# Token table of a mixture of experts: neighbouring places 64 bytes apart, rows gathered with 8 KB

## What is computed

```
logits = xf @ router_w.T                       # 2048 tokens, 8 experts
topk_vals, topk_idx = jax.lax.top_k(logits, 2)
topk_w = jax.nn.softmax(topk_vals, axis=-1)
order = jnp.argsort(exp_id)
x_sorted = xf[order // K]                      # tokens brought together by expert
y1 = ragged_dot(x_sorted, w1, counts); gate, up = split(y1, 2)
y2 = ragged_dot(silu(gate) * up, w2, counts)
y = (y2[inv] * exp_w[:, None]) summed over the 2 experts of a token
```

## Time and profile before

| what | us |
|---|---|
| median of 3 runs | 4060.53 (4059.64 to 4062.84) |
| profiled execution, its own time | 4057.63 |
| its span, first to last instruction | 4055.8 |
| attention of layer 2, first to last shifted scores (L1457) | 1165.5 to 1654.9 |
| scatters of tokens (L1308), first and last issue | 1396.0 and 1691.0 |
| gather of the table's rows (L2033) | 1706.6 |

### The profile page before, as it was taken

The page is one execution under the profiler, slowest core; times in us unless marked ns, Lnnn a source line. Parts: engine busy times, 40 slices in busy tenths (PEclk is TensorE's granted clock), DMA queues, the critical chain, the costliest instruction groups (busy, mean ns, idle before and its releaser), DMA issues.

```text
span 4055.8 us, 35836 instructions
## 1 busy us (share of the span) xinstructions
PE 3666.8 (90%) x11791; PEld 1695.8 (42%) x11792; DVE 2001.4 (49%) x3599; ACT 1370.8 (34%) x2825; POOL 371.0 (9%) x387
## 2 busy tenths in 40 slices
PE   1999999965779899499969999999999999999999
PEld 0444444432434444256524344444444434444443
DVE  8656665153777777311136666665665652111111
ACT  5524342110246666322224344343443431010000
POOL 7000000000212322211110100000000000000000
PEclk6999999987889999799989999999999999999999
DMA  3321312300303232355551100001001002222221
GB/s 117 125 79 59 128 63 68 113 24 11 73 13 74 59 85 52 135 156 166 158 183 45 66 27 33 35 24 35 31 28 36 24 12 78 69 92 83 78 88 52
DMA packets 77705, 291.67 MB, mean 72 GB/s; under 512 B 10728, under 2 KB 11624, under 8 KB 66556
## 3 DMA queue, kind: packets, MB, share of 16 engines
q1 hardware_dynamic: 69216, 264.15, 20.1%
q0 software_dynamic: 8352, 25.78, 2.0%
HBM read 255.73 MB, written 33.64 MB: 71 GB/s over the span
## 4 chain that ended last, share of the span: by engine, by line
PE 78%; DVE 10%; issue 6%; ACT 3%; DMA 2%; POOL 1%; SPq 0%; DVEq 0%; POOLq 0%; ACTq 0%
PE BM L2191 6%; PE BM L2246 5%; PE BM L529 5%; PE BR L529 5%; PE BR L2255 4%; PE BM L364 4%; PE BR L364 4%; PE BS L2229 3%; PE BS L545 3%; PE BT L545 3%; PE BT L2238 3%; PE BR L1887 3%; PE BM L2204 3%; PE BM L1876 2%; PE BR L1876 2%
## 5 line engine op out<-in xcount | busy, mean ns | idle before, releaser
L2320 ACT ACTIVATE AR<-BS,AR 128x512 f32<-128x512 f32 x256 | 174.5, 685 | 412.9 <-DVE AR L2415 412.9
L2314 ACT COPY AR<-BM 128x512 f32<-128x512 f32 x340 | 198.9, 585 | 305.6 <-PE BM L2246 99.9
L2428 DVE SCALAR_TENSOR_TENSOR X<-BR,AR,X 128x512 f32<-128x512 f32 x256 | 191.9, 750 | 206.7 <-PE BR L2255 197.4
L2415 DVE TENSOR_REDUCE AR<-BS 128x2 f32<-128x1024 f32 x128 | 156.9, 1225 | 254.9 <-PE BS L2229 254.9
L2255 PE MATMUL BR<-AR 128*128 128x512 f32 x512 | 255.4, 622 | 4.2 <-DVE X L2428 0.6
L2246 PE MATMUL BM<-AR 128*128 128x512 f32 x512 | 247.0, 595 | 0.0
L2191 PE MATMUL BM<-XT,AR 128*128 128x512 f32 x512 | 236.6, 605 | 0.7 <-ACT XT L239 0.7
L364 PE MATMUL BM<-XT,AR 128*128 (+1 forms) x512 | 231.8, 596 | 4.9 <-DMA AR<-l_w_dram 4.9
L529 PE MATMUL BM<-XT,AR 128*128 128x512 f32 x512 | 231.5, 595 | 0.6 <-ACT AR L632 0.6
L419 DVE TENSOR_TENSOR AR<-AR,BR 128x512 f32<-128x512 f32 x64 | 44.0, 687 | 379.8 <-PE BR L364 379.8
L529 PE MATMUL BR<-XT,AR 128*128 128x512 f32 x512 | 230.2, 592 | 0.0
(11 more groups left out here) (376 smaller groups left out, 5943.7 us busy)
## 6 DMA issues: line engine op xcount, KB each, us to landing
AR<-l_w_dram SPq DMA_DIRECT2D x128, 512.0 KB, 3.5
AR<-l_wq_dram SPq DMA_DIRECT2D x32, 1152.0 KB, 5.1
AR<-l_w_dram SPq DMA_DIRECT2D x42, 768.0 KB, 4.7
AR<-w2h SPq DMA_DIRECT2D x16, 1024.0 KB, 4.8
QS<-qx SPq DMA_DIRECT2D x32, 512.0 KB, 10.0
AR<-l_w_dram SPq DMA_DIRECT2D x16, 1024.0 KB, 4.8
AR<-l_w_dram SPq DMA_DIRECT2D x8, 1408.0 KB
made<-AR SPq DMA_DIRECT2D x40, 256.0 KB, 4.8
```

Of the source, the lines that this page charges most:

```text
L2314: nc.scalar.copy(to, BM[:, L3[job] % 2, :]).then_inc(m_free, 1)
L2428: nc.vector.scalar_tensor_tensor(out=xb, in0=BR[:, L3[job] % 2, :], scalar=RS3[:, p % 2, h, st:st + 1], in1=xb, op0=ALU.mult, op1=ALU.add) ...
```

## The change

Each place of the table gets 16 words, of which only the first is used, so that neighbouring places lie 64 bytes apart and the table has 1 MB instead of 64 KB. The places in IDX0 and IDX1 are written times 16; where VectorE reads them it shifts by 15 bits instead of 11 and multiplies by 1/16. The gather takes rows of 2048 words (8 KB) into an `SLT` 16 times as wide, and the transpose reads every 16th word. The zeros are written by one DMA that repeats the 128 x 32 tile 64 times per partition, in place of four.

```diff
+APART = 16
...
-        table = nc.dram_tensor("table", [P * P, 1], F32, kind="Internal").ap()
+        table = nc.dram_tensor("table", [P * P * APART, 1], F32, kind="Internal").ap()
...
         def route_place(v, b, oh, idx):
             link(v, nc.vector.tensor_tensor(EQ, oh, RT[:, 0:ST, :], ALU.mult))
             link(v, nc.vector.tensor_reduce(POS, EQ, op=ALU.add, axis=AX.X))
-            nc.vector.tensor_copy(idx[:, b * ST:(b + 1) * ST], POS).then_inc(idx_ready, 1)
+            nc.vector.tensor_scalar(idx[:, b * ST:(b + 1) * ST], POS, float(APART), None, ALU.mult).then_inc(idx_ready, 1)
...
-            pool.wait_ge(table_zero, 64)
+            pool.wait_ge(table_zero, 16)
...
-        SLT = a(P)
+        SLT = a(P, APART)
...
             pe.wait_ge(slt_in, 16)
-            nc.tensor.transpose(start_job(pe, er, r)[:, 0:P], SLT, ID[:, :]).then_inc(er.full, 1)
+            nc.tensor.transpose(start_job(pe, er, r)[:, 0:P], SLT[:, :, 0], ID[:, :]).then_inc(er.full, 1)
...
             for idx, yp in ((IDX0, YP0), (IDX1, YP1)):
-                link(v, nc.vector.tensor_scalar(SHIFTED, idx, 11, None, ALU.arith_shift_right))
+                link(v, nc.vector.tensor_scalar(SHIFTED, idx, 15, None, ALU.arith_shift_right))
...
-                link(v, tt(AT_E, AT_E, idx, ALU.add))
+                link(v, nc.vector.scalar_tensor_tensor(out=AT_E, in0=idx, scalar=1.0 / APART, in1=AT_E, op0=ALU.mult, op1=ALU.add))
...
             pool.wait_ge(table_in, 2 * B * ST * 16)
-            nc.gpsimd.indirect_dma_start(out=SLT, out_offset=None, in_=table.rearrange("(r n) o -> r (n o)", n=P),
+            nc.gpsimd.indirect_dma_start(out=SLT.rearrange("p n a -> p (n a)"), out_offset=None, in_=table.rearrange("(r n) o -> r (n o)", n=P * APART),
                                          in_offset=bass.IndirectOffsetOnAxis(ap=ROW, axis=0)).then_inc(slt_in, 16)
...
             sp.wait_ge(zero_ready, 1)
-            for c in range(4):
-                sp.dma_start(table.rearrange("(p n) o -> p (n o)", p=P)[:, 32 * c:32 * c + 32], ZERO[:, :]).then_inc(table_zero, 16)
+            sp.dma_start(table.rearrange("(p a n) o -> p a (n o)", p=P, n=32),
+                         ZERO[:, :].rearrange("p (o n) -> p o n", o=1).to_broadcast([P, P * APART // 32, 32])).then_inc(table_zero, 16)
```

## The result

The changed kernel takes 4036.72 us (median of 6 runs, 4034.78 to 4038.79) against 4059.64 us (6 runs, 4055.08 to 4062.84) for the kernel before in the same series: ratio 0.9945, 95% interval 0.9932 to 0.9958. Profiled execution against profiled execution it is 4038.39 against 4057.63, 19.2 us less.

What follows compares the result with a forecast made beforehand. TensorE is 90% busy, so its idle stretches around the token table, waiting on unconfirmed scatter words, can move. Terms -11.6 - 8.8 + 3.3 = -17.1 from 4060.5 give 4043.4 us; range 4038 to 4065.

Steps and rivals of the forecast that it cites:

- Place and mechanism: Waits behind scatters, at the last batch and in the attention: words sharing 64 B are taken in turn; spacing them cures it.
- Attention: Batches 0 and 1: maxima land before TensorE runs dry, so waits and clock drop go; 7.7 and 1.13, -8.8 us.
- Last scatters: Wait for the table after the last batch's eighth scatter: last one lands 3.27 us after issue, 1694.2 not 1705.83, -11.6 us.
- the other bound: Table wait after the eighth scatter: landing in the maxima's 2.73 us instead, at 1693.7, -12.1 us.
- Gather: Gather of the tokens' rows, now 8 KB each: slower where most partitions read one row; +3.3 us, bounds +1.6 and +4.1.
- Zero fill, transpose, VectorE, third batch: Zeros done by 90, before weights are needed; strided read, same VectorE instructions and freed expert weights cost or gain 0.
- The number: From sum to time: runs' median 2.9 above the profiled 4057.63, so 4060.5 - 17.1 = 4043.4 us.
- case 1: The summed terms hold, stall cured at the last scatters and in the attention: 4041 to 4048 us, chance 0.62.
- Rival 2: Scatters: price hangs on each word, not its neighbour, so only the gather's +3.3 counts; 4063.8 us, chance 0.23.
- Rival 3: Scatters: price per word falls only in part, say to three quarters, 17.6 ns; 4051 us, chance 0.10.
- Rival 4: Start of kernel: 8192 zero pieces at 23.4 ns each delay the first weights, TensorE +102 us late; 4146 us, chance 0.05.

Runs made afterwards that it cites:

- runs by themselves: Two kernels with only scatters, all else left out, output a copy of x, nineteen patterns of 8 x 128 words each; wait 2.17 us where nothing stalls.
- first kernel of scatters: Only scatters, all else left out: one run of places 4 to 4096 B apart, or 8 sections 8 KB to 1 MB apart; first two patterns wait 7.78 and 22.82 us.

## Why the prediction came out as it did

*Place and mechanism: right.* The chain loses the wait behind the eighth scatter, the waits for maxima and the low clock in batch 0's turn, and nothing new takes their place. The runs by themselves show that without neighbours in one 64 B nothing stalls. What the prediction did not have is that the sections' distance sets how much: the edit moves both, and either alone leaves 7.51 or 4.60 us of the 14.88. The reason given, that two words in one 64 B must be taken in turn, is too simple: with eight words per 64 B and sections 16 KB apart the kernel waits 2.64. How the memory treats the words was not seen.

*Attention, predicted -8.8:* -7.69 and -1.12, together -8.8. Taking the pace of two groups from batch 1, with its own small wait taken off, gave the cost of wait and low clock in one. That each batch fits to 0.01 is luck, since the second trace of the kernel before splits the loss as 5.40 and 3.09; the sum, 8.49, is what holds.

*Last scatters, predicted -11.6:* -12.67. The step was "Then the last scatter lands as the nearest indirect DMA does, 3.27 us after its issue". A scatter that nothing stalls lands sooner, 2.21 here and 2.17 in the runs by themselves, so the term was 1.1 us too small, and outside the -12.1 that I gave as the other bound.

*Gather, predicted +3.3:* +2.54, between the bounds +1.6 and +4.1. The step "The nearest row for that is the load of the layer-norm rows (L490), one stretch read from all partitions" was wrong in its reason: with rows of their own the gather lands in the same 5.7 us. So that the two rates gave a sum within 0.8 us is luck. The row itself did not show the reason either, since its 211 GB/s count the packets of all queues. The gather's packets take 3.4 us (1688.3 to 1691.7), 2.5 more than before. By the Trainium skill's 6.15 us for 1 MB and 0.95 for 64 KB (DMA: Bandwidth & Descriptors, section Bandwidth) it would have been +5.2, an estimate; the trace has +2.54, half of that.

*Zero fill, transpose, VectorE, third batch, predicted 0:* the zeros landed at 34.9, where I had allowed them until 90, and nobody waited for the weights. The third batch and VectorE are inside the +0.37, the transpose inside the gather's +2.54.

*The number: the step that failed.* It is the one from the sum to the time, "the runs' median is 2.9 higher, so 4060.5 - 17.1". The terms come to -18.9 instead of -17.1 (the last scatters 1.1 us and the gather 0.8 us mis-sized), which alone gives 4060.5 - 18.9 = 4041.6, inside the range and at the edge of case 1's own 4041 to 4048. The other 4.9 us come from that step: the distance of median and profiled execution was carried over to the changed kernel as if it were a constant. The changed kernel's median lies 1.7 below its profiled execution instead of 2.9 above, 4.6 us of the miss; the last 0.3 are what the two traces differ by beyond the terms. The range had no room for this: its low end lay 5.5 us under the forecast, although the three runs shown already spread by 3.2 us and one profile was all there was. Between the two profiled executions, where this step does not enter, the terms make 18.9 of the 19.2 us.

The number that the step started from moves too. From the later 4051.86 of the kernel before, the same sum gives 4051.86 - 17.1 = 4034.8, where the changed kernel took 4037.11: then the forecast is too low, and the measured 14.8 us are less than the 18.9 that the traces show. So how large the miss is, and even its sign, is in part luck of the series, and the gain in time is known only as 15 to 23 us. Why the kernel before moves by 8 us between series stays open.

*Rival 2* (the price is the word's) falls: with one word per 64 B, 1024 words wait no longer than the floor. With it falls, for this case, the rule of the Trainium skill that was set beside it (DMA: Bandwidth & Descriptors, Specifications): a read-modify-write for every transfer under 512 B may be there, but words of 4 B in 64 B of their own show no price above the pace of issue, 8.84 us from the first scatter to the eighth (68.28 to 77.12 at 64 B in the first kernel of scatters) and then 2.17. *Rival 3* (in part) falls for the whole change; either half of it alone left a part of the stall. *Rival 4* (zero fill) falls by the landing at 34.9.

## What to carry to other kernels

When an engine waits for a scatter while the DMA engines are idle, look at the addresses: small words that share 64 B, written close in time, can be confirmed late, and more so with sections 4 to 128 KB apart in powers of two than in one section. An eighth, a quarter or half of 64 B per word, with the sections moved apart as much, was enough here (2.64 us, and then the floor). Turning the places inside a row together with sections 128 KB apart did it without a larger gather; either alone left 4.60 or 7.51 us. Padding the sections by 512 B was tried only in the scatters by themselves, where it left 5 of 22 us. Before giving a range of a few us around a sum, see how far the profiled execution stands from the median, and how far the median moves from series to series: the kernel before had its median 2.9 us above one profiled execution and 7.5 below another, more than the error in any term.

## What was not expected of the hardware

- Scattered words that are not yet confirmed hold up others' transfers, loads included: maxima 10.77 us, expert weights at 56 GB/s with the DMA engines 1.03 busy, against 315 in the changed kernel. For the maxima the Trainium skill has the rule (DMA: Bandwidth & Descriptors, Queues, rings and completion order): the semaphore increment that ends a transfer lands only after every earlier write of that DMA engine, across its queues. The trace agrees with its 10.77 us, and without the stall TensorE does not wait for them behind scatters at all.
- Eight sections of 4 B words cost 22 us when 8 KB apart, 26 at 16 KB and 5.0 at 8 KB + 512 B.
- 8192 pieces of 128 B, which lie next to one another, do not stall: the zeros have landed 28.8 us after their issue, at most 3.5 ns a piece (an estimate, 28.8 us / 8192), other loads between them.
- A gather of 128 rows of 8 KB lands in 5.7 us whether or not most partitions read one row.
